# Moving copies, inverse roots and column sums between engines and places in a linear-attention and gated-FFN kernel

## The chip, the cores and the metric

One Trainium2 chip, 8 cores, one sequence of the batch on each. Every core runs the same program on its own 2048 rows of 1024 numbers. The time is device microseconds of the slowest core. Engines are named as in the profile: PE is TensorE, ACT is ScalarE, DVE is VectorE, POOL is GpSimd, SP is SyncE, which here only issues DMAs.

## The reference, cut to what matters

```python
# x: (8, 2048, 1024)
x = x + attn(layernorm(x))
x = x + ffn(layernorm(x))

def attn(x, w_qkva, gamma):              # DIM = 1024
    h = rmsnorm(x) * gamma
    q, kv, a = split(einsum('bnd,ed->bne', h, w_qkva), 3)
    a = sigmoid(a)
    y = scan over n of  y_n = a_n * y_(n-1) + kv_n
    return q * y

def ffn(x, W1, b1, W2, b2, Wg, bg):      # 8 experts, hidden size 128
    gate = softmax(x @ Wg + bg)
    h = relu(einsum('bsd,edh->bseh', x, W1) + b1)
    y = einsum('bseh,eho->bseo', h, W2) + b2
    return sum over experts of gate * y
```

## The kernel before, in words

A core's 2048 rows are cut into four chunks of 512 (TC), each into four tiles of 128 rows (NT). Each chunk goes through two phases. `phase_a(c)` computes attention: for each of 8 blocks of 128 output columns (a **group**, j = 0 to 7) three projections of 8 matmuls each: a, kv, q. After the first, ScalarE takes the sigmoid; after the second, VectorE runs the scan (L666) and copies its last column into `carry` (L671); after the third, VectorE multiplies by q (L675: **the product**). The residual is then added: in chunk 0, TensorE transposes the tokens of x into one more bank and VectorE adds (L685: **the add**); in chunks 1 to 3, GpSimd adds (L689). `phase_f(c)` is the FFN: a **quad** (`open_quad`, L733) opens four banks with the bias matmuls, four experts follow (L743, hidden layer, L746 on VectorE), a second quad and four more, and then two quads of output tiles (L762, L765). The order is chunk 0 attention, chunk 1 attention, chunk 0 FFN, chunk 2 attention, chunk 1 FFN, chunk 3 attention, chunk 2 FFN, chunk 3 FFN.

The order of instructions on every engine is written by hand. Each engine is a `Lane` with one queue, run in the order of the calls. `Lane.do(fn, *after)` issues after waiting for the tokens in `after`, and returns a token. Work of other stages is hooked into the phases at named places: in `phase_a`, `(j, 0)` is behind the first projection and the sigmoid of group j, `(j, 1)` behind the second projection, the scan and the carry, and `(j, 2)` behind the product and the add; in `phase_f`, `("h", e)` is behind expert e and `("y", d)` behind output tile d. Hooks of one place run in the order in which they were added.

PSUM has eight banks. Five make a **ring**: `ring_take()` hands them out in turn, and `ring_free[b]` is the token that frees bank b. A group takes three at its start (a, kv, q), in chunk 0 one more for the residual. A quad takes four at once, and its first matmul waits for the tokens of all four:

```python
banks = [ring_take() for _ in range(4)]
free = [ring_free[b] for b in banks]
...
          C[c]["gro"], *free, *after, tick=False)
```

The first layernorm of a chunk (`ln1_*`) works on tokens. `ln1_bn` takes the batch statistics of a tile on VectorE (two halves and one aggregate), `ln1_seed` the first guess of the inverse root of the variance (VectorE, 3 instructions), `ln1_small` three Newton steps and the bias (GpSimd, 14 instructions), `ln1_norm` normalizes one tile (ScalarE, 128x1024). Then the tiles must be turned: for chunk 1 `ln1_turn(1, kp)` does it on TensorE, in four **turns** of 8 transposes (two slices of 128 columns each), all four hooked into group 7 of chunk 0. A turn takes a bank of the ring, and its two copies to SBUF (by VectorE or ScalarE) free it. Chunk 1's first projection reads the slices in their order. For chunks 2 and 3, SP's DMAs transpose (`ln1_turn_dma`), and VectorE multiplies by gamma in place (`ln1_gamma`).

W1's column sums are needed for the bias of the FFN's first layer: `w1_parts` adds up partial sums, and `w1_sums(h)` (h = 0, 1) takes a bank of the ring, folds them with two matmuls, and adds, rounds and combines them in three VectorE instructions (L628, L630, L631). It happens once, in chunk 1's attention. The first FFN quad waits for h = 0, the second for h = 1.

Of the kernel before, what the change touches and what calls it, by code (L numbers as in the profile page):

```python
# [10 lines left out]
ALU = mybir.AluOpType  # L11
# [10 lines left out]
NT = TC // 128  # L22
# [67 lines left out]
def build_program():  # L90
# [14 lines left out]
    with stack:  # L105
# [22 lines left out]
        xn = sb("xn", [128, NT, D], BF16)  # L128
# [22 lines left out]
        va = sb("va", [128, NT], F32)  # L151
        ry = sb("ry", [128, NT], F32)
        ya = sb("ya", [128, NT], F32)
        r1 = sb("r1", [128, NT], F32)
        nb1 = sb("nb1", [128, NT], F32)
        warm = sb("warm", [128, 2], F32)
        bst = sb("bst", [128, NT, 2, 6], F32)
        mv = sb("mv", [128, NT, 2], F32)
# [12 lines left out]
        PE, ACT, DVE, POOL, SP = [Lane(sem(f"s_{n}")) for n in ("pe", "act", "dve", "pool", "sp")]  # L171
# [22 lines left out]
        def load_x0(i):  # L194
# [22 lines left out]
        C = [dict(x2=[None] * KC, xbf=[None] * KC, h=[None] * KC, bn=[None] * NT, xn=[None] * NT,  # L217
                  h1g=[None] * E) for _ in range(NCH)]
# [15 lines left out]
        def ring_take():  # L234
            b = ring["i"] % NRING
            ring["i"] += 1
            return b
# [25 lines left out]
        def ln1_bn(c, i, halves=(0, 1)):  # L263
            for h in halves:
                t = DVE.do(lambda e, h=h: e.bn_stats(  # L265
                    bst[:, i, h, :], tok_of[c][:, i, h * TC:(h + 1) * TC]), xt_t[c][i])
            if 1 in halves:
                C[c]["bn"][i] = DVE.do(lambda e: e.bn_aggr(mv[:, i, :], bst[:, i, :, :].rearrange("p a b -> p (a b)")), t,
                                         C[c - 1]["r1"] if c > 1 else None)

        def ln1_seed(c, lo, hi):

            sl = slice(lo, hi)
            t = DVE.do(lambda e: e.tensor_scalar_max(va[:, sl], mv[:, sl, 1], 9.765625e-33), C[c]["bn"][hi - 1],
                       C[c - 1]["r1"] if c > 1 else C[0]["sd"])
            t = DVE.do(lambda e: e.tensor_scalar(ry[:, sl].bitcast(I32), va[:, sl].bitcast(I32), 1, None,
                                                 ALU.arith_shift_right), t)
            C[c]["seed"] = DVE.do(lambda e: e.tensor_scalar(ry[:, sl].bitcast(I32), ry[:, sl].bitcast(I32), -1.0,  # L278
                                                            1597463007.0, ALU.mult, ALU.add), t)

        def ln1_small(c, lo, hi):

            sl = slice(lo, hi)
            t = C[c]["seed"]
            for it in range(3):
                t = POOL.do(lambda e: e.tensor_tensor(ya[:, sl], ry[:, sl], ry[:, sl], ALU.mult), t)  # L286
                t = POOL.do(lambda e: e.tensor_tensor(ya[:, sl], ya[:, sl], va[:, sl], ALU.mult), t)
                t = POOL.do(lambda e: e.tensor_scalar(ya[:, sl], ya[:, sl], -0.5, 1.5, ALU.mult, ALU.add), t)
                out = r1 if it == 2 else ry
                t = POOL.do(lambda e, out=out: e.tensor_tensor(out[:, sl], ry[:, sl], ya[:, sl], ALU.mult), t,  # L290
                            C[c - 1]["xn"][NT - 1] if it == 2 else None)
            t = POOL.do(lambda e: e.tensor_tensor(nb1[:, sl], mv[:, sl, 0], r1[:, sl], ALU.mult), t)
            C[c]["r1"] = POOL.do(lambda e: e.tensor_scalar(nb1[:, sl], nb1[:, sl], -1.0, None, ALU.mult), t)  # L293

        def ln1_norm(c, i):

            C[c]["xn"][i] = ACT.do(lambda e: e.activation(xn[:, i, :], tok_of[c][:, i, :], AF.Identity,  # L297
                                                          bias=nb1[:, i:i + 1], scale=r1[:, i:i + 1]),
                                   C[c]["r1"], xn_free[i])

        def ln1_turn(c, kp, dve=False):

            b = ring_take()
            pbf = ps[b][:].bitcast(BF16)
            dst = h_of[c]
            for k in (2 * kp, 2 * kp + 1):
                for i in range(NT):
                    off = (k % 2) * TC + i * 128
                    t = PE.do(lambda e, k=k, i=i, off=off: e.matmul(
                        pbf[:, off:off + 128], xn[:, i, k * 128:(k + 1) * 128], identb[:],  # L310
                        start=True, stop=True, is_transpose=True),
                        C[c]["xn"][i], ms["identb"], ring_free[b] if (k % 2 == 0 and i == 0) else None,
                        tick=(k % 2 == 1 and i == NT - 1))
            for k in (2 * kp, 2 * kp + 1):
                src = pbf[:, (k % 2) * TC:(k % 2 + 1) * TC]
                if dve:
                    ev = DVE.do(lambda e, k=k, src=src: e.tensor_scalar_mul(dst[:, k, :], src, gam[:, k:k + 1]), t, gam_t)
                else:
                    ev = ACT.do(lambda e, k=k, src=src: e.activation(dst[:, k, :], src, AF.Copy, scale=gam[:, k:k + 1]),
                                t, gam_t)  # L320
                C[c]["h"][k] = ev
            ring_free[b] = ev
            if kp == 3:
                for i in range(NT):
                    xn_free[i] = t
# [267 lines left out]
        t = DVE.do(lambda e: e.tensor_reduce(fs, ident[:].rearrange("p (r m) -> p m r", m=32), AX.X, ALU.add), id_t)  # L593
# [24 lines left out]
        def w1_sums(h):  # L618


            b = ring_take()
            for k in range(2):
                t = PE.do(lambda e, k=k: e.matmul(ps[b][:], fold[:].rearrange("p r m -> p (r m)"), w1p[h][k],
                                                  start=(k == 0), stop=(k == 1)),
                          w1part[h], fold_t, ring_free[b] if k == 0 else None, tick=(k == 1))
            xn_free[2 * h], xn_free[2 * h + 1] = t, t
            sl = slice(h * 512, (h + 1) * 512)
            t = DVE.do(lambda e: e.tensor_tensor(b1f[:, sl], ps[b][:], b1f[:, sl], ALU.add), t, b1_t)  # L628
            ring_free[b] = t
            t = DVE.do(lambda e: e.tensor_copy(b1h[:, sl], b1f[:, sl]), t)  # L630
            w1b_tok[h] = DVE.do(lambda e: e.scalar_tensor_tensor(  # L631
                w1b[:, 4 * h:4 * h + 4, :].rearrange("p a b -> p (a b)"), b1h[:, sl], nm[:, 0:1], b1f[:, sl],
                ALU.mult, ALU.add), t, nm_t)
            st["h1g"] = w1b_tok[h]
# [159 lines left out]
        def add(hooks, key, fn):  # L794
            hooks.setdefault(key, []).append(fn)
# [14 lines left out]
        def stat_hooks(hooks, c):  # L810

            for k in range(KC - 1):
                add(hooks, (k + 1, 2), lambda k=k: cs_step(c, k))
                if k == 3:
                    add(hooks, (k + 2, 0), lambda k=k: rows_step(c, k))
# [13 lines left out]

        hk = {}  # L830
        for kp, p in enumerate([(7, 1), (7, 1), (7, 2), (7, 2)]):
            add(hk, p, lambda kp=kp: ln1_turn(1, kp, dve=(kp % 2 == 1)))
        stat_hooks(hk, 0)
        gate = {}
        for lo, p in ((0, ((4, 0), (4, 1), (5, 1))), (2, ((5, 0), (5, 1), (6, 1)))):
            add(hk, p[0], lambda lo=lo: (ln1_bn(1, lo), ln1_bn(1, lo + 1)))
            add(hk, p[1], lambda lo=lo: (ln1_seed(1, lo, lo + 2), ln1_small(1, lo, lo + 2)))
            add(hk, p[2], lambda lo=lo: (ln1_norm(1, lo), ln1_norm(1, lo + 1)))
        add(hk, (5, 0), lambda: gate.update(t=gate_sums()))
        phase_a(0, hk)  # L840
        wgs_tok = gate["t"]
# [1 line left out]
        for i in range(NT):  # L843
            load_xt(2, i, C[0]["tx"])

        def bn_hooks(hooks, c):
            for n, p in enumerate([(5, 2), (6, 2), (7, 1), (7, 2)]):
                add(hooks, p, lambda n=n: ln1_bn(c, n))


        hk = {}
# [1 line left out]
        ln2_hooks(hk, 0, A_PLACES)  # L853
        add(hk, (5, 0), w1_parts)
        add(hk, (6, 0), lambda: w1_sums(0))
        add(hk, (6, 1), lambda: w1_sums(1))
        bn_hooks(hk, 2)
        phase_a(1, hk)

        def norm_hooks(hooks, c):  # L860
            add(hooks, ("h", 0), lambda: ln1_seed(c, 0, NT))
            add(hooks, ("h", 0), lambda: ln1_small(c, 0, NT))
            for n in range(NT):
                add(hooks, ("h", 4 + n // 2), lambda n=n: ln1_norm(c, n))
                add(hooks, ("h", 7), lambda n=n: ln1_turn_dma(c, n))
            for k in range(KC):
                add(hooks, ("y", 4 + k // 4), lambda k=k: ln1_gamma(c, k))

        hk = {}
# [5 lines left out]
        hk = {}  # L875
# [5 lines left out]
        hk = {}  # L881
# [3 lines left out]
        hk = {}  # L885
# [4 lines left out]
        hk = {}  # L890
# [76 lines left out]
```

How the kernel before makes its waits and increments, by code:

```python
        def run(eng):  # L52
            for s, v in waits:
                eng.wait_ge(s, v)
            ins = fn(eng)
            if tick:
                ins.then_inc(sem, 1)
# [8 lines left out]
        def run(eng):  # L66
            for s, v in waits:
                eng.wait_ge(s, v)
            fn(eng).then_inc(sem, 16)
# [6 lines left out]
        def run(eng):  # L76
            for s, v in waits:
                eng.wait_ge(s, v)
```

## Time and profile before

| what | us |
|---|---|
| median of 3 runs | 324.97 |
| lowest and highest | 324.45, 325.07 |
| the profiled execution, its own time | 325.49 |
| its span (slowest core, 7) | 323.9 |
| spans of cores 0 to 7 | 321.0, 323.2, 321.1, 323.5, 321.0, 322.9, 321.4, 323.9 |
| TensorE busy on core 7 | 313.2 (97%) |
| VectorE busy | 187.8 (58%) |
| ScalarE busy | 94.3 (29%) |
| GpSimd busy | 62.2 (19%) |
| TensorE's granted clock on core 7 | 0.995 of full speed |

The span runs from the first to the last instruction of a core; the execution's own time is somewhat longer. Times of instructions are counted from the start of the span. A busy time of TensorE holds modelled ends of matmuls: in a stream without gaps, the starts of 128x512 matmuls are 0.216 us apart. "Idle before" is the engine's idle time ahead of an instruction, and the releaser is what ended it.

### The profile page before, as it was taken

The numbers are of one execution on the slowest core, as the hardware profiler recorded it, in microseconds if no ns is written. First come the engines' busy times: TensorE is split into PE (matmuls) and PEld (weight loads), VectorE is DVE, ScalarE is ACT, GpSimd is POOL, SyncE is SP. The second block draws the span as 40 slices with busy tenths as digits, with TensorE's granted clock in tenths as the row PEclk, the third lists the DMA queues.
The fourth block names the chain that finished last, engine by engine and source line by source line (L and its number), as shares of the span: only waits on it lengthen the run. The fifth ranks groups of instructions, "written<-read, shape, count | busy, mean of one in ns | idle before, by whom it ended". The sixth has DMA issues, their size and how long they took to land.

```text
span 323.9 us, 4976 instructions; the slowest of 8 cores (321.0 to 323.9 us)
## 1 busy us (share of the span) xinstructions
PE 313.2 (97%) x1602; PEld 141.6 (44%) x1602; DVE 187.8 (58%) x418; ACT 94.3 (29%) x147; POOL 62.2 (19%) x126
## 2 busy tenths in 40 slices
PE   7699999989999989999999999999999999999996
PEld 3245454454444434444444444444444444444443
DVE  0835387554778994363678784362778346733333
ACT  1472323573245214103236304104235320200000
POOL 4891003311311133001131322001131310000000
PEclk9989999999999999999999999999999999999999
DMA  6999999999993301966900401977000400164023
GB/s 133 206 158 177 220 207 197 223 177 212 207 219 66 132 2 28 168 216 186 274 39 1 131 18 29 170 222 225 10 0 2 144 3 0 51 143 200 0 116 143
DMA packets 21017, 40.93 MB, mean 126 GB/s; under 512 B 11424, under 2 KB 11840, under 8 KB 19968
## 3 DMA queue, kind: packets, MB, share of 16 engines
q1 hardware_dynamic: 16832, 25.87, 28.4%
q0 software_dynamic: 4160, 14.75, 24.9%
q8 instruction: 13, 0.21, 0.3%
q14 instruction: 12, 0.10, 0.1%
HBM read 40.25 MB, written 8.42 MB: 150 GB/s over the span
## 4 chain that ended last, share of the span: by engine, by line
PE 84%; DVE 7%; DMA 3%; issue 3%; ACT 1%; POOL 0%; SPq 0%; DVEq 0%; POOLq 0%; ACTq 0%
PE ps L653 44%; PE ps L743 17%; PE ps L762 17%; DMA xtok<-xt 3%; DVE sc L666 2%; PE ps L733 2%; PE ps L404 1%; PE ps L681 1%; DVE sc L675 1%; DVE bst L265 1%; ACT xn L297 1%; PE ps L710 1%; PE ps L418 1%; PE ps L492 0%; DVE bb L253 0%
## 5 line engine op out<-in xcount | busy, mean ns | idle before, releaser
L653 PE MATMUL ps<-pb,wq 128*128 128x512 bf16 x768 | 170.1, 379 | 0.6 <-DVE pb L524 0.6
L653 PEld LDWEIGHTS ps<-pb,wq 128*128 128x128 bf16 x768 | 74.2, 98 | 90.0 <-issue 4.8
L689 POOL TENSOR_TENSOR xb<-xb,sc 128x512 f32<-128x512 f32 x24 | 30.4, 1268 | 153.6 <-DVE sc L675 114.3
L743 PE MATMUL ps<-pb,w 128*128 128x512 bf16 x256 | 57.0, 380 | 0.0
L762 PE MATMUL ps<-h1g,w 128*128 128x512 bf16 x248 | 55.1, 380 | 0.0
L660 ACT ACTIVATE asig<-ps 128x512 f32<-128x512 f32 x32 | 19.0, 595 | 117.0 <-PE ps L653 98.2
L666 DVE TENSOR_TENSOR_SCAN sc<-asig,carry,ps 128x512 f32<-128x512 f32 x24 | 30.7, 1279 | 30.0 <-PE ps L653 16.6
L765 DVE TENSOR_TENSOR xb<-ps,xb 128x512 f32<-128x512 f32 x31 | 21.4, 691 | 29.6 <-PE ps L762 29.6
L743 PEld LDWEIGHTS ps<-pb,w 128*128 128x128 bf16 x256 | 24.3, 98 | 30.1 <-issue 2.2
L746 DVE SCALAR_TENSOR_TENSOR h1g<-ps,grep 128x512 bf16<-128x512 f32 x32 | 22.1, 692 | 25.9 <-PE ps L743 25.7
L762 PEld LDWEIGHTS ps<-h1g,w 128*128 128x128 bf16 x248 | 23.5, 98 | 29.2 <-issue 2.0
L675 DVE TENSOR_TENSOR sc<-ps,sc 128x512 f32<-128x512 f32 x32 | 22.1, 690 | 5.3 <-PE ps L653 4.6
L391 ACT ACTIVATE pb<-xb 128x512 bf16<-128x512 f32 x32 | 20.0, 625 | 7.5 <-POOL xb L689 7.5
L297 ACT ACTIVATE xn<-xtok,nb,r 128x1024 bf16<-128x1024 f32 x12 | 14.2, 1233 | 25.1 <-POOL nb L293 22.2
L392 ACT ACTIVATE sqr<-xb 128x512 bf16<-128x512 f32 x32 | 19.8, 618 | 0.0
L265 DVE BATCH_NORM_STATS2 bst<-xtok 128x6 f32<-128x512 f32 x24 | 15.7, 684 | 6.3 <-DMA xtok<-xt 6.3
L666 DVE TENSOR_TENSOR_SCAN sc<-asig,ps 128x512 f32<-128x512 f32 x8 | 9.8, 1221 | 14.0 <-PE ps L653 9.6
L463 PE MATMUL ps<-grep 128*128 128x512 bf16 x41 | 11.8, 446 | 1.9 <-DVE grep L190 1.9
L365 ACT ACT_TABLE_LOAD x4 | 5.1, 1283 | 14.0 <-DVE s L363 14.0
L286 POOL TENSOR_TENSOR ya<-ry 128x2 f32<-128x2 f32 (+1 forms) x12 | 2.3, 195 | 30.8 <-DVE ry L278 29.6
L543 POOL DMA_DIRECT2D wq<-wqd x12 | 6.8, 650 | 5.2 <-DMA xtok<-xt 5.2
L463 PEld LDWEIGHTS ps<-grep 128*128 128x128 bf16 x41 | 4.4, 113 | 7.1 <-issue 4.1
(118 smaller groups left out, 172.3 us busy)
## 6 DMA issues: line engine op xcount, KB each, us to landing
xtok<-xt SPq DMA_DIRECT2D x12, 512.0 KB, 10.2
outd<-xb SPq DMA_DIRECT2D x12, 512.0 KB, 4.1
grep<-gscr SPq DMA_DIRECT2D x4, 1024.0 KB, 5.7
xb<-xd SPq DMA_DIRECT2D x8, 512.0 KB, 6.0
wq<-wqd POOLq DMA_DIRECT2D x12, 256.0 KB, 35.3
wq<-wqd POOLq DMA_DIRECT2D x4, 768.0 KB, 21.2
w<-xt POOLq DMA_DIRECT2D x4, 512.0 KB, 32.6
xb<-xd POOLq DMA_DIRECT2D x4, 512.0 KB, 49.3
```

The source lines that it names most:

```text
L265: t = DVE.do(lambda e, h=h: e.bn_stats(bst[:, i, h, :], tok_of[c][:, i, h * TC:(h + 1) * TC]), xt_t[c][i])
L391: t1 = ACT.do(lambda e: e.activation(xbf_of[c][:, k, :], src, AF.Copy), C[c]["x2"][k], prior)
L392: t2 = ACT.do(lambda e: e.activation(sqr[b][:], src, AF.Square), C[c]["x2"][k], sq_free[b])
L653: mm[i] = PE.do(lambda e, k=k: e.matmul(ps[banks[i]][:], wq[:, j, i, k, :], hbc[:, k, :], start=(k == 0), stop=(k == KC - 1)), h[k] if j = ...
L660: sg = ACT.do(lambda e: e.activation(asig[asl][:], ps[ba][:], AF.Sigmoid), mm[0], as_free[asl])
L666: sn = DVE.do(lambda e: e.tensor_tensor_scan(sc[s][:], asig[asl][:], ps[bk][:], init, ALU.mult, ALU.add), sg, mm[1], sc_free[s], st["carry ...
L675: at = DVE.do(lambda e: e.tensor_tensor(sc[s][:], ps[bq][:], sc[s][:], ALU.mult), mm[2], cy)
L689: x2 = POOL.do(lambda e: e.tensor_tensor(xc[:, j, :], xc[:, j, :], sc[s][:], ALU.add), at, x_t[c][j])
L743: t = PE.do(lambda e, k=k: e.matmul(ps[b][:], w1[:, e_, k, :], xbf_of[c][:, k, :], start=False, stop=(k == KC - 1)), C[c]["xbf"][k] if e_ ...
L746: mt = DVE.do(lambda e: e.scalar_tensor_tensor(h1g[:, e_, :], ps[b][:], 0.0, grep[:, e_, :], ALU.max, ALU.mult), t, C[c]["gi"], st["h1g"])
L762: t = PE.do(lambda e, e_=e_: e.matmul(ps[b][:], w2[:, d, e_, :], h1g[:, e_, :], start=False, stop=(e_ == E - 1)), C[c]["h1g"][e_], w2_t[d ...
L765: o = DVE.do(lambda e: e.tensor_tensor(xc[:, d, :], ps[b][:], xc[:, d, :], ALU.add), t, C[c]["cs"][d][1], C[c]["cs"][d][2])
```

## The change

- Chunk 1's turns: before, ScalarE copied turns 0 and 2 and VectorE 1 and 3. After, VectorE copies turn 2 alone, ScalarE the other three.
- Tiles 2 and 3 of chunk 1: the statistics of tile 2 stay at place (5, 0), those of tile 3 move to (5, 1), behind group 5's scan. Seed and roots move from (5, 1) to (5, 2), and the roots are made by VectorE (`ln1_small_dve`, 10 instructions) and no longer by GpSimd (14). The normalization stays at (6, 1). Tiles 0 and 1 keep their order.
- `w1_sums(1)` moves in chunk 1's attention from (6, 1) to (7, 1).
- The statistics of chunk 2's tiles, also in chunk 1's attention, move from (5, 2), (6, 2), (7, 1), (7, 2) to (5, 2), (6, 1), (7, 2), and the fourth into the FFN of chunk 0, behind expert 0. Chunk 2's seed and roots move there from behind expert 0 to behind expert 1. Those of chunk 3 stay.

```diff
--- before.py
+++ after.py
@@ -292,6 +292,20 @@
             t = POOL.do(lambda e: e.tensor_tensor(nb1[:, sl], mv[:, sl, 0], r1[:, sl], ALU.mult), t)
             C[c]["r1"] = POOL.do(lambda e: e.tensor_scalar(nb1[:, sl], nb1[:, sl], -1.0, None, ALU.mult), t)
 
+        def ln1_small_dve(c, lo, hi):
+
+            sl = slice(lo, hi)
+            t = C[c]["seed"]
+            for it in range(3):
+                out = r1 if it == 2 else ry
+                t = DVE.do(lambda e: e.tensor_tensor(ya[:, sl], ry[:, sl], ry[:, sl], ALU.mult), t)
+                t = DVE.do(lambda e: e.scalar_tensor_tensor(ya[:, sl], ya[:, sl], -0.5, va[:, sl], ALU.mult, ALU.mult), t)
+                t = DVE.do(lambda e, out=out: e.scalar_tensor_tensor(out[:, sl], ya[:, sl], 1.5, ry[:, sl], ALU.add,
+                                                                     ALU.mult), t,
+                           C[c - 1]["xn"][NT - 1] if it == 2 else None)
+            C[c]["r1"] = DVE.do(lambda e: e.scalar_tensor_tensor(nb1[:, sl], mv[:, sl, 0], -1.0, r1[:, sl],
+                                                                 ALU.mult, ALU.mult), t)
+
         def ln1_norm(c, i):
 
             C[c]["xn"][i] = ACT.do(lambda e: e.activation(xn[:, i, :], tok_of[c][:, i, :], AF.Identity,
@@ -829,13 +843,15 @@
 
         hk = {}
         for kp, p in enumerate([(7, 1), (7, 1), (7, 2), (7, 2)]):
-            add(hk, p, lambda kp=kp: ln1_turn(1, kp, dve=(kp % 2 == 1)))
+            add(hk, p, lambda kp=kp: ln1_turn(1, kp, dve=(kp == 2)))
         stat_hooks(hk, 0)
         gate = {}
-        for lo, p in ((0, ((4, 0), (4, 1), (5, 1))), (2, ((5, 0), (5, 1), (6, 1)))):
-            add(hk, p[0], lambda lo=lo: (ln1_bn(1, lo), ln1_bn(1, lo + 1)))
-            add(hk, p[1], lambda lo=lo: (ln1_seed(1, lo, lo + 2), ln1_small(1, lo, lo + 2)))
-            add(hk, p[2], lambda lo=lo: (ln1_norm(1, lo), ln1_norm(1, lo + 1)))
+        for lo, p, small in ((0, ((4, 0), (4, 0), (4, 1), (5, 1)), ln1_small),
+                             (2, ((5, 0), (5, 1), (5, 2), (6, 1)), ln1_small_dve)):
+            add(hk, p[0], lambda lo=lo: ln1_bn(1, lo))
+            add(hk, p[1], lambda lo=lo: ln1_bn(1, lo + 1))
+            add(hk, p[2], lambda lo=lo, small=small: (ln1_seed(1, lo, lo + 2), small(1, lo, lo + 2)))
+            add(hk, p[3], lambda lo=lo: (ln1_norm(1, lo), ln1_norm(1, lo + 1)))
         add(hk, (5, 0), lambda: gate.update(t=gate_sums()))
         phase_a(0, hk)
         wgs_tok = gate["t"]
@@ -843,8 +859,8 @@
         for i in range(NT):
             load_xt(2, i, C[0]["tx"])
 
-        def bn_hooks(hooks, c):
-            for n, p in enumerate([(5, 2), (6, 2), (7, 1), (7, 2)]):
+        def bn_hooks(hooks, c, places=((5, 2), (6, 2), (7, 1), (7, 2))):
+            for n, p in enumerate(places):
                 add(hooks, p, lambda n=n: ln1_bn(c, n))
 
 
@@ -853,13 +869,15 @@
         ln2_hooks(hk, 0, A_PLACES)
         add(hk, (5, 0), w1_parts)
         add(hk, (6, 0), lambda: w1_sums(0))
-        add(hk, (6, 1), lambda: w1_sums(1))
-        bn_hooks(hk, 2)
+        add(hk, (7, 1), lambda: w1_sums(1))
+        bn_hooks(hk, 2, ((5, 2), (6, 1), (7, 2)))
         phase_a(1, hk)
 
         def norm_hooks(hooks, c):
-            add(hooks, ("h", 0), lambda: ln1_seed(c, 0, NT))
-            add(hooks, ("h", 0), lambda: ln1_small(c, 0, NT))
+            if c == 2:
+                add(hooks, ("h", 0), lambda: ln1_bn(c, NT - 1))
+            add(hooks, ("h", 3 - c), lambda: ln1_seed(c, 0, NT))
+            add(hooks, ("h", 3 - c), lambda: ln1_small(c, 0, NT))
             for n in range(NT):
                 add(hooks, ("h", 4 + n // 2), lambda n=n: ln1_norm(c, n))
                 add(hooks, ("h", 7), lambda n=n: ln1_turn_dma(c, n))
```

## Rows read from the trace of the kernel before

**Rows 1.** TensorE in order: start us, us, what xcount [idle before <-releaser]

```profile
60.53 3.62 PE L653 MATMUL ps<-pb,wq 128*128 128x512 bf16 x16
63.99 0.33 PE L309 MATMUL ps<-identb,xn 128*128 128x128 bf16 x3
64.81 0.89 PE L309 MATMUL ps<-identb,xn 128*128 128x128 bf16 x13 [0.49 <-ACT xn L297]
65.53 1.89 PE L653 MATMUL ps<-pb,wq 128*128 128x512 bf16 x8
...
67.72 0.61 PE L309 MATMUL ps<-identb,xn 128*128 128x128 bf16 x8
69.41 0.61 PE L309 MATMUL ps<-identb,xn 128*128 128x128 bf16 x8 [1.08 <-DVE sc L675]
69.85 7.07 PE L653 MATMUL ps<-pb,wq 128*128 128x512 bf16 x32
```

**Rows 2.** VectorE's instructions in order, from 52 to 69 us

```profile
52.10 1.29 DVE L265 BATCH_NORM_STATS2 bst<-w 128x6 f32<-128x512 f32 x2 [1.39 <-DMA w<-xt]
...
53.62 1.26 DVE L265 BATCH_NORM_STATS2 bst<-w 128x6 f32<-128x512 f32 x2
...
55.26 1.22 DVE L666 TENSOR_TENSOR_SCAN sc<-asig,ps 128x512 f32<-128x512 f32 x1
...
56.65 0.16 DVE L274 TENSOR_SCALAR va<-mv 128x2 f32<-128x2 f32 x1
...
57.30 0.69 DVE L675 TENSOR_TENSOR sc<-ps,sc 128x512 f32<-128x512 f32 x1
58.09 0.69 DVE L685 TENSOR_TENSOR xb<-ps,sc 128x512 f32<-128x512 f32 x1
58.70 1.22 DVE L666 TENSOR_TENSOR_SCAN sc<-asig,ps 128x512 f32<-128x512 f32 x1
...
60.44 0.69 DVE L675 TENSOR_TENSOR sc<-ps,sc 128x512 f32<-128x512 f32 x1 [0.26 <-PE ps L653]
...
66.36 1.22 DVE L666 TENSOR_TENSOR_SCAN sc<-asig,ps 128x512 f32<-128x512 f32 x1 [4.43 <-ACT asig L660]
...
68.58 0.68 DVE L675 TENSOR_TENSOR sc<-ps,sc 128x512 f32<-128x512 f32 x1
```

**Rows 3.** ScalarE's instructions in order, from 62 to 69 us

```profile
62.29 2.37 ACT L297 ACTIVATE xn<-w,nb,r 128x1024 bf16<-128x1024 f32 x2 [3.76 <-POOL nb L293]
...
68.43 1.26 ACT L319 ACTIVATE pb<-ps,cst 128x512 bf16<-128x512 bf16 x2 [1.09 <-PE ps L309]
```

**Rows 4.** all engines in order, chunk 1's last groups to the quad

```profile
107.85 7.12 PE L653 MATMUL ps<-pb,wq 128*128 128x512 bf16 x32
...
108.77 1.27 DVE L666 TENSOR_TENSOR_SCAN sc<-asig,carry,ps 128x512 f32<-128x512 f32 x1
...
112.26 0.69 DVE L675 TENSOR_TENSOR sc<-ps,sc 128x512 f32<-128x512 f32 x1
...
114.48 1.28 DVE L666 TENSOR_TENSOR_SCAN sc<-asig,carry,ps 128x512 f32<-128x512 f32 x1
...
115.90 0.40 PE L733 MATMUL ps<-gro,w1b 32*128 32x512 bf16 x4 [0.93 <-DVE sc L666]
```

**Rows 5.** all engines in order, from 92 to 95 us

```profile
92.84 1.26 POOL L689 TENSOR_TENSOR xb<-xb,sc 128x512 f32<-128x512 f32 x1 [3.85 <-DVE aa L252]
...
92.87 1.25 DVE L253 SCALAR_TENSOR_TENSOR bb<-aa,vv 128x4 f32<-128x4 f32 x1
...
94.76 0.16 DVE L253 SCALAR_TENSOR_TENSOR bb<-aa,vv 128x4 f32<-128x4 f32 x1
...
95.03 0.16 DVE L257 SCALAR_TENSOR_TENSOR r<-bb,rr 128x4 f32<-128x4 f32 x1
```

**Rows 6.** all engines in order, chunk 0's FFN, from 125 to 141 us

```profile
125.92 4.64 ACT L297 ACTIVATE xn<-xtok,nb,r 128x1024 bf16<-128x1024 f32 x4 [10.26 <-POOL nb L293]
...
140.87 1.13 DVE L336 TENSOR_SCALAR pb<-pb,cst 128x512 bf16<-128x512 bf16 x4
```

## The prediction

> **What bounds the kernel now.** I read the page first (its engine table: TensorE busy 97% of the span), then the cores (core 7 is the slowest), then TensorE's waits, and then each wait's neighbourhood in the timeline. All below is core 7. With TensorE that full, a gain can only come out of its gaps, and a loss only by making new ones. After the head of the kernel the waits of TensorE name three places, all in the part that the change touches.
>
> Gap A and B stand between chunk 0 and chunk 1 [rows 1]. TensorE reaches the first turns at 63.99, stops after 3 transposes and goes on at 64.81, when ScalarE has the last normalized tile. Three transposes take 0.165 at 0.055 each, so the stream loses 0.65 (the row's 0.49 is less, since the ends of matmuls are modelled; I count starts throughout). Then turn 3 starts at 69.41, while turn 2 has been issued by 67.72 + 0.44 = 68.16: 1.25 lost. From 60.53, where group 7 of chunk 0 starts, to 69.85, where chunk 1 starts, it is 9.32.
>
> Why turn 3 waits: PSUM banks are handed out in a ring of five, so it takes the bank of group 7's third projection, freed by the product at 68.58 [rows 2]. That product follows a scan at 66.36, which waited 4.43 for ScalarE's sigmoid. The sigmoid stood in ScalarE's queue behind two normalizations that began at 62.29, when GpSimd had the inverse roots [rows 3]. Between scan and product stand the carry's copy and the two copies of turn 1.
>
> Gap C stands between chunk 1's projections and the first FFN quad [rows 4]. TensorE starts 32 matmuls at 107.85, 6.91 at 0.216 each, and would be free at 114.76. The quad starts at 115.90, 1.14 late, held by group 7's scan (start 114.48). Again the ring: the quad takes four banks and its first matmul waits for all; the last to come free is the second projection's.
>
> **The change, chunk 0.** I follow VectorE's queue with its own spacings.
> - The batch statistics of tile 2 still start at 52.10, because their data land then. A pair with its aggregate takes 1.52 (52.10 to 53.62) [rows 2]. Now tile 3's stand behind group 5's scan instead of ahead of it. The gate's sum (0.15) goes at 53.62, the scan at 53.77, tile 3's statistics 1.39 later (as 55.26 to 56.65) at 55.16, the product at 56.67, the add at 57.46 (0.79 on, as 57.30 to 58.09), and the seed at 58.07 (0.61 on, as 58.09 to 58.70).
> - Seed and roots: 3 + 10 dependent instructions. The trace has their kind at 94.76 and 95.03, 0.27 apart, 0.16 long [rows 5]. The last starts at 58.07 + 12 x 0.27 = 61.31 and ends at 61.47; normalization starts at about 61.55 instead of 62.29 [rows 3], 0.74 earlier.
> - The price: group 6's scan stands behind them. It goes at 61.56 instead of 58.70 [rows 2]. Scan to product is 1.58 (1.39 for the carry, and some 0.2), so the product is at 63.14 and the add to the residual from 63.93 to 64.62. In the ring, turn 0 takes the bank that this product frees (63.83 plus 0.15 for TensorE to see it, 63.98: just in time for 63.99), and turn 1 takes the bank that the add frees, at 64.77, while TensorE wants it at 64.43. Gap A, 0.65, becomes a gap of 0.33 with another releaser. The normalized tiles are ready at 61.55 + 2.37 + 0.15 = 64.07, in time for the fourth transpose at 64.15. The third projection starts at 65.21 instead of 65.53.
> - Sigmoid and scan of group 7 move with the normalization: scan at 66.36 - 0.74 = 65.62. Turn 1's copies are no longer on VectorE (0.88 between carry and product gone), so VectorE could give the product at 67.20. It also needs the third projection: the row at 60.44 shows a product starting 0.09 before the next group's 60.53, and turn 2, which follows like that group, is now at 67.72 - 0.32 = 67.40. So 67.31. It ends at 67.99, turn 3 starts at 68.14 instead of 69.41, and chunk 1's first matmul at 68.58 instead of 69.85: 1.27 gained.
> - The copies that changed engine: turn 2's now start on VectorE behind the add, at 68.71, and turn 3's on ScalarE 0.71 after turn 3 starts (as 67.72 to 68.43 [rows 1, 3]), at 68.85, two in 1.26, the last ending 70.11. TensorE wants the eighth slice at 68.58 + 7 x 0.216 = 70.09. It may stand 0.1 there, 0 to 0.4 as bounds. Gain 1.2.
>
> Bounds of this gain: 1.6 if the add came in time (0.33 more and no stall at the copies). If the ten root instructions took GpSimd's kind of pace, some 0.34 (a chain of 14 there stretches from the seed's end near 57.4 to the normalization at 62.29 [rows 2, 3]), 0.7 comes off: 0.5.
>
> **The change, chunk 1.** The second half of W1's sums (two matmuls, 0.43, and three VectorE instructions) moves from group 6 to group 7, one tile's statistics move into group 6, another into the FFN.
> - VectorE's queue up to group 6's scan (108.77) keeps its place relative to TensorE. Then, in time of before: a tile's statistics 110.2 to 111.8, product 6 at 111.8 instead of 112.26, free at 112.4 [rows 4].
> - TensorE, without the two matmuls, starts group 6's third projection at 107.42, group 7 at 109.15, and has issued two of its projections by 112.60. Scan 7 needs the second, and starts at about 112.9 instead of 114.48: 1.6 earlier. So far this would close gap C.
> - But between this scan and product 7 now stand W1's three instructions, and the ring has moved by one: the sum's bank is taken after group 7's, not before. The quad's four banks are then those of the first sum and of all three projections of group 7, so its first matmul waits for product 7. Scan to product with these three between was 108.77 to 112.26, 3.49 [rows 4]. So product 7 runs 116.4 to 117.05, and the quad starts at 117.2 instead of 115.90: a loss of 1.3. Bounds: 1.1 to 1.5, by a scan 0.2 to either side.
> - Costed at nothing: the last tile's statistics (1.5), the seeds one expert later. Queued behind are the products of experts 0 and 1 (the second perhaps 0.4 late; the second quad needs only expert 2's bank). The roots on GpSimd and the four normalizations come about 2.1 later than their 125.92 to 130.56, then the four transposing DMAs on SP; VectorE first reads the result at 140.87, 1.3 later now [rows 6]. That is 10 of cover, less 0.8.
>
> **A rule weighed.** A VectorE operation over 128x4 took 1.25 where it started 0.03 behind GpSimd's 1.26 add, and its like took 0.16 alone [rows 5]. GpSimd does nothing while the ten new instructions run here, and its add of group 6 in chunk 1 falls beside a scan, whose rows are 1.27 to 1.28 throughout. The Trainium skill, "SBUF — State Buffer", section "Who interferes with whom", says that a VectorE instruction with two SBUF inputs and a GpSimd one that reads SBUF exclude each other; the row agrees. By a collision the sum would be 1.1 worse; without one it stands.
>
> **The sum.** 323.9 - 1.2 + 1.3 = 324.0 for the span, and 1.6 outside it as in the profiled execution (325.49): 325.6, 0.1 over its own. The median of the runs is 324.97, so 325.1. The other three slow cores have the same gap C; they don't change which core ends last by more than tenths.
>
> **The rivals.** Within 0.2% (0.65) no measurement of this kernel tells a change from none.
> - My forecast: the gain at the chunk boundary is handed back at the quad. 324.5 to 325.6. Chance 0.52.
> - Slower: the roots' chain on VectorE slips. From gap A on, each tenth that the add of group 6 comes later is a tenth that TensorE loses, with nothing to absorb it. At 0.34 a piece the gain is 0.5 and the time 325.8; with a collision as in rows 5 it is 326.2. It decides from a slip of 0.55. For it: the path is serial, and turn 0's bank has 0.01 to spare. Against: the 0.27 is measured on like shapes. Chance 0.30.
> - Faster: the quad doesn't wait for product 7 but for scan 7, as now. Then it starts when TensorE is free, at 114.34, and the time is 324.97 - 1.2 - 1.56 = 322.2. For it: that is what the trace names now. Against: the count of banks. Chance 0.06.
> - Faster, smaller: the boundary gives 1.6 and the quad loses only 0.9 (W1's three instructions quicker, the product earlier): 324.3. Chance 0.12.
>
> Likeliest alone 324.5 to 325.6; the range 324.0 to 326.0 leaves out the bank miscounted and a collision. Faster 0.18, same 0.52, slower 0.30.
>
> **What would show it.** In the profile after: TensorE's wait before the turns names the add of group 6 (0.2 to 0.4) rather than ScalarE; turn 3's wait falls from 1.08 to about 0.1 to 0.3; the quad's wait names the product with the third projection instead of the scan, and is about 2.2 instead of 0.93. The gap from group 7's start in chunk 0 to chunk 1 falls from 9.32 to 8.1. If the quad's wait is under 1, the forecast is wrong on the fast side; if the turns wait a microsecond, on the slow side.

## The result, and the profile after

The changed kernel took 326.69 us (median of four), the kernel before beside it 324.71: a ratio of 1.0064, 95% interval 1.0051 to 1.0076. It is slower, by 2.1 us where 0.1 was forecast, and outside the range of 324.0 to 326.0.

The cores of the profiled execution of the changed kernel, with their span and mean granted clock:

```profile
core 0: 325.2 us, clock 0.995
core 1: 324.9 us, clock 0.993
core 2: 323.7 us, clock 1.000
core 3: 323.2 us, clock 1.000
core 4: 322.1 us, clock 1.000
core 5: 323.8 us, clock 1.000
core 6: 323.4 us, clock 1.000
core 7: 323.2 us, clock 1.000
```

Six cores end between 322.1 and 323.8, which is where the forecast put the kernel (324.0 for the slowest). Two end 1.1 to 1.4 later, and they are the two with a clock below 1. In each of the four executions the slowest core was one with 0.993 to 0.995; only the profiled one shows where in the kernel its clock was low.

TensorE in order on core 0, at the boundary between chunks 0 and 1 and then ahead of the first FFN quad. L667 are the projections, L323 the turns, L695 chunk 0's transposes, L637 W1's sums, L747 the quad, L757 the experts:

```profile
60.07 3.62 PE L667 MATMUL ps<-pb,wq 128*128 128x512 bf16 x16
63.52 1.06 PE L323 MATMUL ps<-identb,xn 128*128 128x128 bf16 x16
64.42 1.89 PE L667 MATMUL ps<-pb,wq 128*128 128x512 bf16 x8
66.14 0.60 PE L695 MATMUL ps<-cst,xtok 128*128 128x128 f32 x4
66.58 1.35 PE L323 MATMUL ps<-identb,xn 128*128 128x128 bf16 x16
67.77 7.23 PE L667 MATMUL ps<-pb,wq 128*128 128x512 bf16 x32
...
103.33 0.59 PE L637 MATMUL ps<-xn,fold 128*128 128x512 bf16 x2
103.77 7.07 PE L667 MATMUL ps<-pb,wq 128*128 128x512 bf16 x32
111.00 0.59 PE L637 MATMUL ps<-xn,fold 128*128 128x512 bf16 x2 [0.16 <-DVE sc L689]
111.43 1.89 PE L667 MATMUL ps<-pb,wq 128*128 128x512 bf16 x8
115.33 0.40 PE L747 MATMUL ps<-gro,w1b 32*128 32x512 bf16 x4 [2.02 <-DVE sc L689]
115.66 8.77 PE L757 MATMUL ps<-pb,w 128*128 128x512 bf16 x32
```

Beside [rows 1]: from 60.07 to 67.77 it is 7.70, where before it was 9.32 on core 7, and no wait is left in the 16 transposes of turns 0 and 1. Beside [rows 4]: the quad starts 12.00 after the first W1 sum, where the kernel before has 10.64 on every core; its wait is 2.02 idle and ends with the product L689, as forecast. What was not forecast is the last row: 32 expert matmuls take 8.77. On the six other cores the same 32 take 7.08.

Stretches of 4 us of core 0, then of core 7 (columns: stretch and its length; busy time and instructions of PE, PEld, DVE, ACT, POOL; then the granted clock, DMA share, GB/s):

```profile
111.00:115.00 4.00, 2.31 (x10) 0.88 (x10) 3.67 (x6) 1.15 (x2) 1.27 (x1) 1.00 0.01 4
115.00:119.00 4.00, 3.67 (x13) 1.41 (x14) 1.59 (x4) 0.00 (x0) 1.27 (x1) 0.61 0.00 0
119.00:123.00 4.00, 4.00 (x20) 1.73 (x19) 3.29 (x9) 0.00 (x0) 0.16 (x1) 0.96 0.00 0
```

```profile
111.00:115.00 4.00, 1.97 (x12) 0.69 (x10) 3.68 (x7) 1.15 (x2) 0.98 (x2) 1.00 0.00 0
115.00:119.00 4.00, 4.00 (x23) 1.88 (x20) 2.81 (x6) 0.00 (x0) 0.94 (x1) 1.00 0.00 0
119.00:123.00 4.00, 4.00 (x22) 1.59 (x21) 2.56 (x7) 0.00 (x0) 1.38 (x7) 1.00 0.00 0
```

Core 0 issues 13 matmuls from 115 to 119 where core 7 issues 23. Slice by slice its granted clock is 1.00 until 115, 0.93, then 0.50 for three slices of 1 us, 0.86, and 1.00 again: it fell from 2.4 to 1.2 GHz right behind the wait. Both cores had waited equally long. The Trainium skill, "TensorE: Matmul & The Clock Gate", section "What's actually happening", says that the clock depends on how busy the array has been, between just these two rates; the trace agrees.

### The profile page after: what moved, and what is told of

Same layout as the page of the kernel before. It is cut to its first block, busy times and chain, and to the rows that moved or that the text cites. A ratio compares the mean times of both kernels' runs of the same rounds, so it can differ in the third digit from the quotient of the medians.

```text
span 325.2 us, 4969 instructions; the slowest of 8 cores (322.1 to 325.2 us)
## 1 busy us (share of the span) xinstructions
PE 314.4 (97%) x1602; PEld 141.5 (44%) x1602; DVE 188.4 (58%) x426; ACT 95.5 (29%) x149; POOL 59.5 (18%) x112
## 4 chain that ended last, share of the span: by engine, by line
PE 92%; DVE 3%; DMA 2%; ACT 1%; issue 1%; DVEq 0%; ACTq 0%
PE ps L667 51%; PE ps L757 18%; PE ps L776 17%; DMA xtok<-xt 2%; PE ps L747 2%; PE ps L418 1%; ACT xn L311 1%; PE ps L695 1%; DVE bst L265 1%; PE ps L323 1%; PE ps L724 1%; PE ps L432 1%; DVE sc L680 0%; PE ps L623 0%; DVE h1g L642 0%
## 5 line engine op out<-in xcount | busy, mean ns | idle before, releaser
L667 PE MATMUL ps<-pb,wq 128*128 128x512 bf16 x768 | 170.2, 379 | 0.6 <-DVE pb L538 0.6
L667 PEld LDWEIGHTS ps<-pb,wq 128*128 128x128 bf16 x768 | 74.2, 98 | 90.0 <-issue 5.1
L757 PE MATMUL ps<-pb,w 128*128 128x512 bf16 x256 | 58.7, 387 | 0.0
L680 DVE TENSOR_TENSOR_SCAN sc<-asig,carry,ps 128x512 f32<-128x512 f32 x24 | 30.7, 1278 | 30.5 <-PE ps L667 17.6
L757 PEld LDWEIGHTS ps<-pb,w 128*128 128x128 bf16 x256 | 24.7, 99 | 31.4 <-issue 4.4
L689 DVE TENSOR_TENSOR sc<-ps,sc 128x512 f32<-128x512 f32 x32 | 22.0, 689 | 6.3 <-PE ps L667 5.0
L680 DVE TENSOR_TENSOR_SCAN sc<-asig,ps 128x512 f32<-128x512 f32 x8 | 9.8, 1220 | 11.1 <-PE ps L667 10.0
L286 POOL TENSOR_TENSOR ya<-ry 128x4 f32<-128x4 f32 (+1 forms) x9 | 1.8, 197 | 31.8 <-DVE ry L278 31.0
```

What stands on the lines that cost most here:

```text
L667: mm[i] = PE.do(lambda e, k=k: e.matmul(ps[banks[i]][:], wq[:, j, i, k, :], hbc[:, k, :], start=(k == 0), stop=(k == KC - 1)), h[k] if j = ...
L680: sn = DVE.do(lambda e: e.tensor_tensor_scan(sc[s][:], asig[asl][:], ps[bk][:], init, ALU.mult, ALU.add), sg, mm[1], sc_free[s], st["carry ...
L689: at = DVE.do(lambda e: e.tensor_tensor(sc[s][:], ps[bq][:], sc[s][:], ALU.mult), mm[2], cy)
L757: t = PE.do(lambda e, k=k: e.matmul(ps[b][:], w1[:, e_, k, :], xbf_of[c][:, k, :], start=False, stop=(k == KC - 1)), C[c]["xbf"][k] if e_ ...
```

## The experiments

The times stand beside the kernel before on the same chip; "ratio" is of these two.

**Is it the clock?** Nine matmuls whose result nobody reads (L888), ahead of the quad, writing a PSUM bank that is free then. The output is that of the changed kernel.

```diff
+        for i in range(9):
+            PE.do(lambda e: e.matmul(ps[5][:], wq[:, 7, 2, 7, :], wq[:, 0, 0, 0:4, :], start=True, stop=True),
+                  psR_free[0] if i == 0 else None, tick=False)
         hk = {}
         norm_hooks(hk, 2)
         phase_f(0, hk)
```

> The changed kernel with nine unused 128x512 matmuls put ahead of chunk 0's first FFN quad, where TensorE otherwise waits 2.0 us for product 7 (they write a PSUM bank that nobody reads then, 9 x 0.216 = 1.9 us, less than the 2.17 between the last projection and the quad). Theory 1 (the clock): the wait itself costs what was forecast, and what makes the change slower is that after it the granted clock falls to half on one or two cores, and the slowest core is one of them. Then no core shows a drop at the quad, the quad starts at the same distance from the first sum (12.0 us), and the median is about 1.7 under the changed kernel's: 324.7 to 325.1, ratio to the kernel before 0.999 to 1.001. Theory 2 (the drop has nothing to do with the wait, or the drop is not what sets the slowest core): cores still show 0.993 to 0.995 and the median stays at 326.5, ratio 1.005 to 1.007.

Measured: 325.67 against 324.77, ratio 1.0032 (1.0021 to 1.0042). TensorE in order on its slowest core:

```profile
111.62 1.89 PE L667 MATMUL ps<-pb,wq 128*128 128x512 bf16 x8
113.34 2.11 PE L888 MATMUL ps<-wq 128*128 128x512 bf16 x9
115.51 0.40 PE L747 MATMUL ps<-gro,w1b 32*128 32x512 bf16 x4
115.84 7.08 PE L757 MATMUL ps<-pb,w 128*128 128x512 bf16 x32
```

The quad stands where it stood (12.00 behind the first sum on every core), the idle is filled, and the experts take 7.08 on all eight cores; in the profiled execution all clocks are 0.999 or 1.000. Of the seven others, one has a core at 0.995, and it is the slowest there (325.0, time 326.56); where its clock fell is not on record. Against the changed kernel's ratio it is 0.0032, or 1.0 us, better. Theory 1 holds in kind; 1.0 and not 1.7, since the cores with a drop need not be those that come to the quad last (in the changed kernel 115.33 on core 0, which ends at 325.2, and 115.73 on core 5, which has no drop and ends at 323.8). And the median is 0.6 above the range that I expected: 1.0 over the kernel before is left, which the clock does not explain.

**Does a wait alone do it?** The kernel before, and one more wait.

```diff
+                C[c]["at"] = at
...
-                banks = open_quad(lambda n: w1b[:, n, :], q, w1b_tok[q // 4])
+                banks = open_quad(lambda n: w1b[:, n, :], q, w1b_tok[q // 4], C[1]["at"])
```

> The kernel before with one edit: the first FFN quad of chunk 0 also waits for product 7 of chunk 1 (in the trace of before it ends at 118.15, the quad starts at 115.90). Nothing else moves, so the wait grows from 0.93 to about 3.3 us. Theory 1 (a long idle of TensorE lets its granted clock fall): 2.4 for the wait itself and 1.7 for a drop on the slowest core: 324.8 + 2.4 + 1.7 = 328.9, range 328.3 to 329.6, and cores with a mean clock of 0.993 to 0.995 and first experts at 0.5 of full clock. Theory 2 (the drop came with something else in the change): 327.0 to 327.4, no core below full clock at the quad.

Measured: 329.9 against 324.93, ratio 1.0148 (1.0128 to 1.0168). Some of the cores, and the stretches around the quad on the slowest, 1:

```profile
core 1: 327.4 us, clock 0.989
core 2: 327.2 us, clock 0.995
core 3: 323.7 us, clock 1.000
...
core 6: 326.4 us, clock 0.988
```

```profile
113.00:117.00 4.00, 0.68 (x6) 0.21 (x6) 3.79 (x8) 0.75 (x2) 0.62 (x1) 0.81 0.00 0
117.00:121.00 4.00, 4.00 (x10) 1.41 (x11) 0.93 (x3) 0.00 (x0) 0.64 (x1) 0.50 0.00 0
121.00:125.00 4.00, 4.00 (x17) 1.64 (x16) 1.51 (x5) 0.00 (x0) 1.64 (x9) 0.83 0.00 0
```

The wait is 3.32 idle and the quad is 2.4 later, as worked out. The clock fell on seven of eight cores, in the wait or right behind it, and the 32 experts take 8.5 to 9.7 there: up to 2.6 more, so the time is 0.3 above the range. The two cores with 2.6 more, 1 and 6, were at 0.50 of the clock when the quad started. The wait alone makes the drop, in a kernel that holds nothing else of the change. Counting cores whose experts slowed: two of eight with 2.02 idle (the changed kernel), three with 2.34 (next run), seven with 3.32, each in one profiled execution; and none of 48 with 0.93, in the six profiled executions that have it. The mean clocks of all the executions behind the ratios order the same way: below 0.998 are 7 of 32 cores in the changed kernel, 20 of 40 in the next run, 30 of 32 here, and 1 of 64 with the unused matmuls. The kernel before has 22 of 416 in the executions beside these runs, so a mean clock alone does not say that the quad was the place.

**Chunk 1's part alone.** The changed kernel with chunk 0's hooks of before.

```diff
-            add(hk, p, lambda kp=kp: ln1_turn(1, kp, dve=(kp == 2)))
+            add(hk, p, lambda kp=kp: ln1_turn(1, kp, dve=(kp % 2 == 1)))
...
-                             (2, ((5, 0), (5, 1), (5, 2), (6, 1)), ln1_small_dve)):
+                             (2, ((5, 0), (5, 0), (5, 1), (6, 1)), ln1_small)):
```

> Chunk 1's part alone (W1's second sum, chunk 2's statistics and seed), chunk 0 as before. Theory 1: the quad's wait is 2.0, it costs 1.4 against before, and on some cores the clock falls behind it for another 1.7: 324.7 + 1.4 + 1.7 = 327.8, range 327.2 to 328.3, with one or more cores at 0.993 to 0.995 and a quad of experts of 8.7 us there. Theory 2: 326.0 to 326.3, no drop at the quad.

Measured: 327.11 against 324.77, ratio 1.0070 (1.0058 to 1.0083). The first sum to the quad is 12.00 on all cores, and three cores dropped (experts 8.35, 8.41, 8.77). The kind is that of theory 1, the size 0.7 less than I said, 0.1 under the range: in the profiled execution the slowest core (324.8) was one that came late to the quad (116.07) and had no drop.

**Chunk 0's part alone.** The changed kernel with W1's sum, chunk 2's statistics and its seed at their places of before.

```diff
-        add(hk, (7, 1), lambda: w1_sums(1))
-        bn_hooks(hk, 2, ((5, 2), (6, 1), (7, 2)))
+        add(hk, (6, 1), lambda: w1_sums(1))
+        bn_hooks(hk, 2)
...
-            if c == 2:
-                add(hooks, ("h", 0), lambda: ln1_bn(c, NT - 1))
-            add(hooks, ("h", 3 - c), lambda: ln1_seed(c, 0, NT))
-            add(hooks, ("h", 3 - c), lambda: ln1_small(c, 0, NT))
+            add(hooks, ("h", 0), lambda: ln1_seed(c, 0, NT))
+            add(hooks, ("h", 0), lambda: ln1_small(c, 0, NT))
```

> Chunk 0's part of the change alone (copies, roots on VectorE, tile 3's statistics); W1's sums and chunk 2's statistics and seed at their places of before. If the two parts add up: from chunk 0's group 7 to chunk 1's start 7.7 us instead of 9.3 on the slowest core, gap C as before (0.93 idle), no drop: 324.7 - 1.6 + 0.2 = 323.3, range 322.8 to 323.9. On the rival view, that which core is slowest is set in the head and the boundary gain is only that of the slowest, it would be 323.9 to 324.4.

Measured: 324.66 against 324.77, ratio 0.9995 (0.9985 to 1.0005): no gain that can be told, and above both ranges. The boundary is 7.69 to 7.70 on all eight cores, as expected, and gap C has its 0.93. But the quad stands 11.00 behind the first sum, not 10.64, on all eight. VectorE in order on its slowest core (L685 is the carry's copy, L689 product 5 of chunk 1):

```profile
103.25 0.15 DVE L685 COPY carry<-sc 128x1 f32<-128x1 f32 x1
103.86 0.69 DVE L689 TENSOR_TENSOR sc<-ps,sc 128x512 f32<-128x512 f32 x1 [0.46 <-DVE carry L685]
```

At the same place the kernel before has 0.25 from the copy to the product:

```profile
104.35 0.15 DVE L671 COPY carry<-sc 128x1 f32<-128x1 f32 x1
104.60 0.69 DVE L675 TENSOR_TENSOR sc<-ps,sc 128x512 f32<-128x512 f32 x1
```

TensorE had issued that third projection more than a microsecond earlier, so 0.36 is lost on VectorE with nobody to wait for, on the loaded stretch that ends with scan 7 and the quad.

**Where does this stop come from?** The same kernel with 36 tiny memsets on VectorE, 12 each into its idle time behind groups 0, 1 and 2 of chunk 0 (its lines are numbered one higher: L686 is the copy, L690 the product).

```diff
+        spare = sb("spare", [128, 36], F32)
...
+        def fill(j):
+            for i in range(12 * j, 12 * j + 12):
+                DVE.do(lambda e, i=i: e.memset(spare[:, i:i + 1], 0.0), tick=False)
+
+        for j in range(3):
+            add(hk, (j, 2), lambda j=j: fill(j))
         phase_a(0, hk)
```

> Chunk 0's part alone again, with 36 tiny memsets of VectorE put into its idle time in groups 0 to 2 of chunk 0. In the run of chunk 0's part alone the quad stood 11.00 behind the first W1 sum on every core instead of 10.64, because product 5 of chunk 1 started 0.61 after the carry's copy instead of 0.25. Theory 3 (VectorE stops for some 0.4 us at certain counts of instructions, and the eight added instructions moved such a stop onto the loaded stretch ahead of the quad): with 36 more instructions the stop falls elsewhere, the distance is 10.64 again, and the time is 0.2 to 0.4 below that of chunk 0's part alone: 324.3 (324.0 to 324.6). Rival (something that runs at that moment, such as a DMA or another engine, holds VectorE there): the distance stays 11.00 and the time 324.7.

Measured: 324.2 against 324.93, ratio 0.9979 (0.9969 to 0.9989), and 10.64 on all cores. VectorE on core 0 at the same place:

```profile
102.46 0.15 DVE L686 COPY carry<-sc 128x1 f32<-128x1 f32 x1
102.72 0.69 DVE L690 TENSOR_TENSOR sc<-ps,sc 128x512 f32<-128x512 f32 x1
```

More instructions made the kernel faster. The gap is gone from this place although the other engines do there what they did, so the stop goes with VectorE's own stream. This is also the size of chunk 0's part freed of it: 0.7.

**Chunk 0's two halves.** First only the copies, on the kernel before.

```diff
-            add(hk, p, lambda kp=kp: ln1_turn(1, kp, dve=(kp % 2 == 1)))
+            add(hk, p, lambda kp=kp: ln1_turn(1, kp, dve=(kp == 2)))
```

> The kernel before with only the copies moved (ScalarE copies turns 0, 1 and 3, VectorE turn 2). On cores whose tile 2 lands late, product 7 no longer stands behind turn 1's copies, which is worth up to 0.6 to 0.7 at the boundary; on the others 0.1, of which the last copies on ScalarE take some back (0.16 in chunk 1's first matmuls of the changed kernel). Two VectorE instructions fewer, so the stop of 0.4 stays off the stretch ahead of the quad (10.64). Time 324.4 to 324.8, ratio 0.9985 to 1.0. Rival: the whole gain of chunk 0's part comes from the roots, and this run is 324.8 to 325.1.

Measured: 325.25 against 325.37, ratio 0.9993 (0.9984 to 1.0001). Then the run of chunk 0's part alone with the copies put back:

```diff
-            add(hk, p, lambda kp=kp: ln1_turn(1, kp, dve=(kp == 2)))
+            add(hk, p, lambda kp=kp: ln1_turn(1, kp, dve=(kp % 2 == 1)))
```

> Only the roots on VectorE and tile 3's statistics behind group 5's scan, the copies as before. Eight VectorE instructions more (ten in all with the copies back), so if the stop goes by the count of instructions it lies within two of where it lay, near product 5 of chunk 1, and the distance from the first sum to the quad is 10.9 to 11.0 again; the boundary's distance is 7.7 to 8.0 on all cores, since it no longer hangs on when tile 2's data land. Time 324.3 to 324.8. Rival for the stop: it sits elsewhere and the distance is 10.64.

Measured: 325.01 against 325.37, ratio 0.9991 (0.9982 to 1.0000). The stop in both, VectorE in order on the slowest core, the copies' run first (L671 the carry's copy, L628 the first instruction of the second W1 sum), then the roots' run (L680 the scan):

```profile
109.52 0.15 DVE L671 COPY carry<-sc 128x1 f32<-128x1 f32 x1
109.99 0.69 DVE L628 TENSOR_TENSOR h1g<-ps,h1g 128x512 f32<-128x512 f32 x1 [0.32 <-issue]
```

```profile
102.25 1.27 DVE L680 TENSOR_TENSOR_SCAN sc<-asig,carry,ps 128x512 f32<-128x512 f32 x1
103.99 0.15 DVE L685 COPY carry<-sc 128x1 f32<-128x1 f32 x1 [0.46 <-DVE sc L680]
```

With ten instructions more than before the stop is ahead of group 5's carry; with eight more, one instruction later, ahead of product 5; with two fewer, nine later again, ahead of the W1 sum. I had expected two fewer to keep it off this stretch, and that was wrong: the distance to the quad is 11.00 in both runs. By this row, the kernel before should have it near group 6's scan, where its own rows show no gap; whether it is covered by the long instruction ahead of it was not tried. Neither half alone can be told from no change; each carries the 0.36 of the stop.

The boundary is 7.69 to 7.70 on six cores of the copies' run, and 8.12 and 8.20 on the two whose tile 2's statistics started only 9.00 and 8.93 ahead of group 7. In the roots' run it is 7.82 to 7.88 on seven cores, and 8.33 on the one with 8.67. So each half removes a part of what late data cost, and I was wrong that the roots alone make it 7.7 to 8.0 on all cores.

**The kernel before once more.**

> The kernel before, profiled once more, for the boundary between chunk 0 and chunk 1. If what the prediction took from core 7 is typical of the slowest core, its distance from group 7 of chunk 0 to chunk 1 is again 9.0 to 9.3. If it was one execution's accident of when tile 2's data landed, it is 7.8 to 7.9 on most or all cores, and the change has only 0.1 to 0.2 to gain there; chunk 0's part alone measured the same as before, which speaks for that.

Measured: 324.87. The first row is VectorE's start of tile 2's statistics on its slowest core, 2, the second the same on core 0 of the changed kernel:

```profile
51.44 1.29 DVE L265 BATCH_NORM_STATS2 bst<-w 128x6 f32<-128x512 f32 x2 [0.71 <-DMA w<-xt]
```

```profile
50.47 1.28 DVE L265 BATCH_NORM_STATS2 bst<-w 128x6 f32<-128x512 f32 x2 [0.23 <-DMA w<-xt]
```

From group 7 of chunk 0 to the first W1 sum this execution has 43.2 on four cores, 43.4 to 43.6 on three and 44.0 on core 2. The first profile of the kernel before had 43.2 to 43.3 on four, and 43.9, 44.3, 44.6, 44.7 on the others, core 7 the worst. The changed kernel has 43.26 everywhere. Over the cores of these two profiles the boundary follows the time from tile 2's statistics to group 7: 7.8 where they start 9.9 ahead, 8.0 at 9.7, 8.5 at 9.3, 8.6 at 9.1, 8.85 at 8.9, 9.15 at 8.6 and 9.32 at 8.43. So the loss at the boundary is real, and it hangs on when tile 2's data land: 0 on half of the cores, 0.8 on the slowest here, 1.5 on the one that I had read. The boundary of its slowest core is 8.63, between the two values that I had set against each other.

**The bank outside the ring.** The changed kernel, but the second W1 sum uses bank 5 of PSUM.

```diff
-            b = ring_take()
+            b = ring_take() if h == 0 else 5
+            free = ring_free[b] if h == 0 else psR_free[0]
...
-                          w1part[h], fold_t, ring_free[b] if k == 0 else None, tick=(k == 1))
+                          w1part[h], fold_t, free if k == 0 else None, tick=(k == 1))
...
-            ring_free[b] = t
+            if h == 0:
+                ring_free[b] = t
+            else:
+                psR_free[0] = t
```

> The changed kernel, but the second W1 sum takes a PSUM bank outside the ring, so the quad gets the banks it had and waits for scan 7, not for product 7. Theory 1: the quad's wait falls from 2.0 to 0.0 to 0.2, no clock drop, and the whole gain of the chunk boundary stays: 324.7 - 1.6 - 1.1 = 322.0, range 321.6 to 322.6, ratio 0.990 to 0.994. Rival (the quad would be held by something else in VectorE's queue, such as the sum itself): the wait stays at 1 to 2 and the time is 323.1 to 326.

Measured: 323.53 against 324.77, ratio 0.9965 (0.9952 to 0.9978). The quad's wait is gone, 9.59 to 9.60 behind the first sum instead of 12.00. But the time is 1.5 above what I worked out: the boundary is worth 0.7 and not 1.6, and VectorE's backlog shows up one quad later. The second quad starts 7.92 to 7.93 behind the first on every core, where the kernel before has 7.34. TensorE on its slowest core (L751 the quads, L761 the experts, L764 the hidden layer on VectorE):

```profile
113.70 0.39 PE L751 MATMUL ps<-gro,w1b 32*128 32x512 bf16 x4
114.03 7.08 PE L761 MATMUL ps<-pb,w 128*128 128x512 bf16 x32
121.63 0.40 PE L751 MATMUL ps<-gro,w1b 32*128 32x512 bf16 x4 [0.52 <-DVE h1g L764]
```

**The best of both.** That kernel, with chunk 2's third tile's statistics behind expert 0, the fourth's behind expert 2, and the seed behind expert 3.

```diff
-        bn_hooks(hk, 2, ((5, 2), (6, 1), (7, 2)))
+        bn_hooks(hk, 2, ((5, 2), (6, 1)))
...
-                add(hooks, ("h", 0), lambda: ln1_bn(c, NT - 1))
-            add(hooks, ("h", 3 - c), lambda: ln1_seed(c, 0, NT))
-            add(hooks, ("h", 3 - c), lambda: ln1_small(c, 0, NT))
+                add(hooks, ("h", 0), lambda: ln1_bn(c, NT - 2))
+                add(hooks, ("h", 2), lambda: ln1_bn(c, NT - 1))
+            at = ("h", 3 if c == 2 else 0)
+            add(hooks, at, lambda: ln1_seed(c, 0, NT))
+            add(hooks, at, lambda: ln1_small(c, 0, NT))
```

> The changed kernel with the second W1 sum's bank outside the ring, and chunk 2's third and fourth tile statistics and its seed moved on to behind experts 0, 2 and 3 of chunk 0's FFN. In the run with the bank alone, the quad had no wait, but the second quad waited 0.51 idle for expert 2's product on VectorE, and the time was 323.5. If that is the whole of what was given back: the second quad's wait is gone and the time is 323.0, range 322.7 to 323.3, ratio to before 0.993 to 0.996. Rival (a later stage gives it back): 323.4 to 323.7 though the wait is gone.

Measured: 323.25 against 324.93, ratio 0.9947 (0.9933 to 0.9961). It beats both kernels and lies inside the range. TensorE on its slowest core, no wait at either quad:

```profile
111.39 1.89 PE L671 MATMUL ps<-pb,wq 128*128 128x512 bf16 x8
113.21 0.40 PE L751 MATMUL ps<-gro,w1b 32*128 32x512 bf16 x4
113.54 7.08 PE L761 MATMUL ps<-pb,w 128*128 128x512 bf16 x32
120.55 0.39 PE L751 MATMUL ps<-gro,w1b 32*128 32x512 bf16 x4
```

## Why the prediction was wrong, by its own steps

- **Gap A and the roots.** Right in kind. The ten instructions run 0.27 apart, and no collision with GpSimd came. The predicted wait of 0.33 for the add did not: tile 2's statistics started 9.60 ahead of group 7 on core 0 (50.47 and 60.07), where the core that I had read had 8.43. So the upper bound of the step, 1.6, seems to be what the boundary showed (7.70 for 9.32), but that compares a core with late data to cores with earlier ones: no core in the profile of the changed kernel had less than 9.48, and the kernel before has 8.19 at 9.55. Whether the add would hold TensorE on a core as late as 8.43 no run shows. Against the gain stand 0.16 in the matmuls after it (7.23 for 7.07). They are the price of the last copies, which I had put at 0.1: the run of the copies alone has them, that of the roots alone does not.
- **Gap C, the ring.** Right: the quad waits for product 7, and it costs 1.36 (12.00 for 10.64), forecast 1.3. The rival "the bank miscounted" is excluded, and the run with the bank outside the ring shows that the count is the cause. That rival's own sum was off by 0.4: its 114.34 left out the sum's two matmuls, which still run ahead of the quad. With them TensorE is free at 114.76, and the run with the bank outside the ring has 9.59 behind the first sum, 114.85 by the times of core 7.
- **The sum: two steps failed.** First, "a loss of 1.3" took the longer wait at its length. It also has a price behind it. The stage costs 1.7 more on each core on which the clock falls, and in the time of the slowest that was 1.0. This was in none of the rivals. The kernel before had its sign, though not in a row that I showed: its core 7 had a mean clock of 0.995. That drop lies in the head of the kernel, from 14.9 on, behind two waits of 2.22 and 0.83 (columns as above):

```profile
12.00:16.00 4.00, 2.68 (x21) 1.62 (x22) 3.41 (x11) 2.39 (x6) 4.00 (x9) 0.85 1.02 139
16.00:20.00 4.00, 3.34 (x22) 1.70 (x20) 1.46 (x7) 2.75 (x5) 4.00 (x9) 0.72 1.03 144
```

On core 3 of the same execution waits of 2.26 and 0.59 at these places were followed by a clock of 1.00. In the head it costs little, as TensorE waits for others anyway (chunk 0's projections start at 19.91 on core 7 and at 19.80 on core 3); ahead of a full stream the same event has a price.
- **Second, 1.2 for the boundary was the gain of one core in one execution.** Freed of the stop, chunk 0's part measured 0.7, and as the change makes it, 0.2 with an interval that includes no change. The loss that it removes came with data that land late on some cores and not on others, and a program over eight cores is as fast as its slowest, which is then another one.
- **The stop of 0.36** was in no step either. In chunk 0's part alone it took half of the gain. In the changed kernel it is there too, ahead of product 5, but costs nothing at the quad: chunk 1's part alone has no such stop, its scan 7 waits 0.50 for TensorE where the changed kernel's waits 0.16, and the quad is 12.00 behind the first sum in both.
- Put together from the parts as measured: -0.7 at the boundary, +1.36 at the quad, +1.0 by the clock, 1.7 against the 2.1 (1.7 to 2.5) measured. The 0.4 between has no row of its own, but it is not outside the noise: the first term alone has an interval of 0.4 to 1.0. The run without a drop has the same remainder: 0.7 from the parts, 1.0 (0.7 to 1.4) measured. The best version closes: -0.7 and -1.05 (9.59 for 10.64) make 1.75, measured 1.7.

## What to carry to other kernels

A wait of TensorE is not priced by its length alone: once it is longer than the others of its kind, look at the granted clock in the stretch behind it, on every core, and price it by what the slow cores lose. When work that takes a buffer of a ring is moved, count the ring again at the next place that takes several at once; a buffer of its own for the rare user was worth 2.4 us at the quad here. And a gain read off one core that waits for data should be looked for on all cores and in a second execution before it goes into a sum.

## What the runs showed of the hardware that was not expected

- A wait of 2.0 us let the clock fall on two cores of eight, and one of 3.3 on seven, with the same program and the same idle time on every core; 0.93 did so on none of 48. A drop cost 1.3 to 1.7 us, and 2.6 on two cores at the longest wait, whose clock had fallen before it ended.
- VectorE stops for about 0.4 us at places that go roughly with its count of instructions: with ten more, eight more and two fewer than before, the stop lay at three places, one and then nine instructions further on, and 36 more took it off the stretch. What it is was not tried, and at the place where the count would put it in the kernel before no gap shows. Where it falls on a chain that the critical engine waits for, it moved the quad by 0.36, and 36 unrelated instructions moved the time by about 0.5, between two intervals that just touch.
